# Twelve tiles of the last count on GpSimd and ScalarE, an early first norm, a separate tile for the first mixture's norms, a third bank for the last experts, and a refitted timetable

## The chip, the cores and the metric

One NeuronCore of a Trainium2 chip runs the whole program. The metric is the device time of one execution in microseconds. The engines are TensorE (PE; PEld is its weight load), VectorE (DVE), ScalarE (ACT), GpSimd (POOL) and SyncE (SP), each with its own in-order instruction stream; they meet only in semaphores.

## The reference, cut to what matters

Eight batches (B = 8) of 512 rows of 128 numbers go through two layers. Each layer has a modulation `mod` from `c @ wmod` and is x + gate * f(scale * norm(x) + shift), twice. In short:

```python
# layer 0, attention: 8 heads of 16
scores = q @ k.T * 0.25 * 1.25
threshold = top_k(scores, 102)[0][..., -1:]          # per row, the 102nd largest
scores *= where(scores >= threshold, 1.24, 1.0)
li = conv3(scores.mean(axis=-2))                      # one factor per key and head
ctx = softmax(scores * li) @ v;  out = ctx @ Wo + bo
# layer 0, mixture: x = res + n + (n @ mix_w + mix_b), then 8 experts, top 2 by softmax
y_e = silu(n @ w1[e] + b1[e]) @ w2[e] + b2[e];  out = sum_e combine[:, e] * y_e
# layer 1, state space: in_proj, conv4, silu, x_proj, softplus; 512 steps of
h = exp(dt * A) * h + dt * b * x;  y = h . c + D * x   # 256 channels x 16 states
# layer 1, mixture: top 2 of 8 experts, at most 153 rows an expert, rows gathered and scattered
y_e = (gelu-like)(x @ w_gate[e]) * (x @ w_c_fc[e]) @ w_c_proj[e]
```

The threshold of each of 32 tiles (8 heads x 4 blocks of 128 queries, 128 x 512 scores each) is found by search: a tile's scores are compared with a guess, the hits of each row are counted, and the guess is moved. After three rounds the fourth and last count leaves the number of scores at or over the last guess and the mask of them.

## The kernel before

The work is written as 29 small threads (Python generators), each bound to one engine, each running over the eight batches. `weave` (L2096) puts them into the engines' streams: it keeps a planned clock for each engine, takes the time after each `yield` of a number as the duration of what was just issued and a `yield` of a semaphore value as a wait, and always issues the piece with the earliest planned start. Of pieces that start within `NEAR` of each other the one that is due first by `TIMETABLE` (L50) goes first. So the order on each engine is fixed when the program is built, by planned and not by real times.

A batch goes through these stages:

- prepare: `dve_norm` (L485; statistics, reciprocal root on GpSimd by `pool_norm`, normalised tile), `pe_prepare` and `act_prepare` for keys, queries and values. Queries and keys are split into three bf16 parts each (`dve_prepare`), written to memory and read back stacked (`sp_stack`).
- refill: `pe_refill`, `act_refill`: 32 score tiles, scaled by each row's length, as f16 (`z_at`).
- search: `act_search` (L776) and `dve_search` (L790), four rounds. In rounds 0, 1, 2 ACT does 8, 14, 14 of the 32 tiles with Sign and a sum, DVE the others; in the fourth (k = 3) DVE does all 32 (`SIGNS`, L39).
- choice: `pe_choice`, `dve_choice`, `pool_choice`: the exact threshold and mask weights, 32 tiles.
- softmax: `pe_softmax`, `act_softmax`, `dve_softmax`, then `pe_project`; `attended` ends attention.
- mixture 0: `dve_mixture0` (L1269), `pe_mixture0`, `act_mixture0`: three norms in bank `side`, router, split; then `pe_experts0`, `act_experts0`, `pool_experts0`: 32 expert steps, in each a matmul up, Silu on ACT, a product on POOL (L1413), a matmul down.
- states: `dve_mamba`, `dve_states` and partners: 32 scans.
- mixture 1: `dve_mixture1` routes, `pool_mixture1` scatters the rows of `rest.nrm` to memory with eight indirect DMAs (L1765, signal `sent_in`), `pe_mixture1` reads them back turned; `pe_experts1` (L1777), `act_experts1`, `dve_experts1`: 32 steps over two banks; then `res_rows`, store, eight gathers on POOL (`pool_finish`, L1897), and `dve_finish` (L1887) adds them and sends the batch out.

Attention of one batch runs beside everything behind attention ("rest") of the batch before. Both have their own banks (`att.bank`, `rest.bank`) and tiles, each four banks of 128 x 512 f32. All three norms of mixture 0 and both of layer 1 write the same tile `rest.nrm`; so `dve_mixture0` waits for `shares` and `sent_in` of the batch before, and `pe_mixture0` for `tok`.

Before the threads start, `sp_setup`, `pool_setup`, `act_setup`, `pe_setup` (L389) and `dve_setup` (L398) run: loads in SP's queue, constants, both layers' modulation; `started` (L460) makes each engine wait for all of it. `pool_one_hots` stands first in `pool_rest`, with a planned 20.0.

Of the kernel before, what the change touches and what calls it, by code (L numbers as in the profile page):

```python
# [11 lines left out]
B, S, D = 8, 512, 128  # L12
P = 128
# [25 lines left out]
SIGNS = (8, 14, 14, 0)  # L39
SLOPE = 1.0 / 140.0  # L40
# [8 lines left out]
PERIOD = 363.6  # L49
TIMETABLE = {  # L50
    "pe_rest": (155.6425, (1727.5, 3672.5, 2524.5)),
    "act_rest": (83.2100, (3233.2, 3240.1, 2778.8)),
    "dve_rest": (110.8225, (2583.4, 3814.2, 3934.2)),
    "pool_rest": (118.1500, (0.0, 1840.0, 357.8)),
    "sp_rest": (15.3000, (3830.8, 3231.2, 5913.4)),
    "pe_mixtures": (10.3100, (4106.7, 4650.2, 5749.5)),
    "act_mixtures": (2.7000, (2555.5, 2487.3, 2054.2)),
    "dve_mixtures": (18.7400, (2279.9, 3457.5, 4617.6)),
    "pool_mixtures": (3.1800, (3586.9, 4341.6, 4427.8)),
    "dve_finishes": (2.8800, (6003.9, 4512.4, 4461.6)),  # L60
    "pool_finishes": (9.0400, (4205.9, 3170.0, 4019.7)),
    "sp_finishes": (0.9000, (5331.9, 7065.6, 6229.8)),
    "pe_choices": (42.2400, (2470.1, 2031.9, 620.0)),
    "act_choices": (2.5600, (4613.2, 4593.8, 3374.6)),
    "dve_choices": (58.8100, (1867.1, 2951.7, 2585.9)),
    "pool_choices": (21.4400, (2700.2, 3240.7, 4358.6)),
    "pe_attention": (57.4700, (4549.4, 4490.0, 4186.3)),
    "act_attention": (76.9400, (3555.2, 3778.3, 4824.6)),
    "dve_attention": (104.6500, (5209.4, 3457.4, 3015.7)),
    "pool_attention": (6.4600, (3316.0, 4230.4, 5170.6)),  # L70
    "sp_attention": (10.3500, (3385.9, 2184.6, 2995.6)),
    "pe_prepares": (9.0800, (2715.0, 4201.9, 1888.5)),
    "act_prepares": (2.9000, (5207.8, 5106.6, 2033.5)),
    "dve_prepares": (16.2500, (7193.4, 6820.5, 7496.6)),
    "pe_refills": (12.8000, (3056.0, 3617.0, 4283.2)),
    "act_refills": (19.2000, (1273.8, 220.9, 1809.4)),
    "sp_rows": (0.3937, (3488.0, 2251.9, 2327.0)),
    "sp_ups": (10.6875, (5049.3, 5188.3, 4982.0)),
    "sp_downs": (7.0875, (5306.5, 3602.3, 3452.1)),
# [51 lines left out]
def emit(nc, ctx, A, out):  # L131
# [40 lines left out]
    siluc, modp, bop, ready = sig("siluc", 2), sig("modp", 2), sig("bop"), sig("ready", 5)  # L172
# [98 lines left out]
    aim, signed, counted = sig("aim", ROUNDS), sig("signed", sum(SIGNS)), sig("counted")  # L271
# [30 lines left out]
    hid = [flat(hfc2)[:, wide + u * CAP:wide + (u + 1) * CAP] for u in range(2)]  # L302
# [4 lines left out]
    ccs = [sb(f"ccs{i}", [P, S]) for i in range(3)]  # L307
    spreadsBC = nc.dram_tensor("spreads", (2 * NS, S), F32, kind="Internal").ap()
# [36 lines left out]
    def pool_setup():  # L345
# [26 lines left out]
        built.up(pool.iota(spare[:], pattern=[[P, PICKS]], base=SLOTS, channel_multiplier=1))  # L372

# [1829 lines left out]
```

## Time and profile before

| | us |
|---|---|
| median of three timed runs | 2922.21 (2920.47 to 2929.23) |
| the profiled execution | 2924.21 |
| its span, first to last instruction | 2923.0 |
| busy: PE / DVE / ACT / POOL | 2182 / 2338 / 1463 / 1190 |

The mean granted clock of TensorE was 0.874 of full speed. The profile gives busy time by engine; the chain that ended last, followed back from the last instruction; groups of instructions by line, with the idle time before them and what released them; and instructions in order of time. A TensorE instruction of f32 counts as two passes (x2). The durations that overlap the next instruction's start are pipelined: a count on DVE is 742 ns long, but the next one starts 667 ns after it.

### The profile page before, as it was taken

The numbers are of one execution on the slowest core, as the hardware profiler recorded it, in microseconds if no ns is written. First come the engines' busy times: TensorE is split into PE (matmuls) and PEld (weight loads), VectorE is DVE, ScalarE is ACT, GpSimd is POOL, SyncE is SP. The second block draws the span as 40 slices with busy tenths as digits, with TensorE's granted clock in tenths as the row PEclk, the third lists the DMA queues.
The fourth block names the chain that finished last, engine by engine and source line by source line (L and its number), as shares of the span: only waits on it lengthen the run. The fifth ranks groups of instructions, "written<-read, shape, count | busy, mean of one in ns | idle before, by whom it ended". The sixth has DMA issues, their size and how long they took to land.

```text
span 2923.0 us, 33653 instructions
## 1 busy us (share of the span) xinstructions
PE 2182.0 (75%) x8767; PEld 1101.9 (38%) x8767; DVE 2338.2 (80%) x6145; ACT 1463.2 (50%) x3124; POOL 1189.6 (41%) x1118
## 2 busy tenths in 40 slices
PE   4169776978778876888679876888769887778645
PEld 2016222553234522554235522454235532355214
DVE  5884898979898798978998798978989788953472
ACT  2406723766166733767056742757146751644323
POOL 2020253615454253725445152724445163724461
PEclk8589798999989998989989999989989898789757
DMA  4001112242043312233033321333133321313223
GB/s 107 0 15 36 29 37 85 80 107 75 27 122 71 104 50 72 91 96 93 27 107 75 105 60 54 109 78 103 31 97 83 101 63 39 113 38 111 83 75 95
DMA packets 137459, 215.11 MB, mean 74 GB/s; under 512 B 17872, under 2 KB 57440, under 8 KB 134112
## 3 DMA queue, kind: packets, MB, share of 16 engines
q1 hardware_dynamic: 133088, 203.88, 24.2%
q0 software_dynamic: 4096, 8.40, 0.9%
q14 instruction: 204, 1.67, 0.2%
q8 instruction: 71, 1.16, 0.2%
HBM read 190.06 MB, written 22.15 MB: 73 GB/s over the span
## 4 chain that ended last, share of the span: by engine, by line
DVE 35%; issue 19%; PE 19%; POOL 10%; ACT 9%; DVEq 4%; DMA 3%; SPq 1%; POOLq 0%; ACTq 0%
DVE wmask L804 10%; DVE best L946 6%; DVEq L948 4%; POOL gat L1649 4%; PE ps_att L1064 3%; ACT wmask L786 2%; POOL slots L1765 2%; PE ps_rest L1353 2%; PE ps_rest L1439 2%; PE ps_att L1075 2%; PE ps_rest L1792 1%; DVE pick L953 1%; POOL rest_c L1662 1%; POOL rest_c L1649 1%; DVE hg L1621 1%
## 5 line engine op out<-in xcount | busy, mean ns | idle before, releaser
L1413 POOL TENSOR_TENSOR gat<-sil,cbs 128x512 f32<-128x512 f32 x256 | 324.4, 1271 | 137.0 <-ACT sil L1378 74.2
L1378 ACT ACTIVATE sil<-ps_rest,w_b1T 128x512 f32<-128x512 f32 x256 | 175.3, 685 | 383.3 <-PE ps_rest L1353 369.9
L804 DVE TENSOR_SCALAR_CACHE_REDUCE wmask<-z,tc 128x512 bf16<-128x512 f16 x512 | 345.8, 742 | 18.3 <-ACT z L771 15.6
L980 POOL TENSOR_SCALAR wmask<-wmask 128x512 bf16<-128x512 bf16 x256 | 158.2, 618 | 412.4 <-DVE wmask L937 409.2
L1064 PE MATMUL ps_att<-z,Vp 128*32 128x128 f32 x2048 | 277.3, 280 | 13.1 <-DVE z L1136 13.1
L1353 PE MATMUL ps_rest<-rest_hT,WF 128*128 128x512 f32 x512 | 281.5, 636 | 0.0
L1343 PE MATMUL ps_rest<-gat,WP 128*128 128x512 f32 x512 | 269.3, 608 | 15.6 <-POOL gat L1413 15.4
L737 PE MATMUL ps_att<-qk 128*128 128x512 bf16 x512 | 227.8, 465 | 45.7 <-DMA qk<-bounce 27.1
L1064 PEld LDWEIGHTS ps_att<-z,Vp 128*32 128x32 f32 x2048 | 206.4, 111 | 124.5 <-issue 115.1
L1592 ACT ACTIVATE ps_rest<-cols,Aneg 128x512 f32<-128x512 f32 x256 | 173.3, 681 | 100.6 <-DVE hg L1621 91.2
L1075 PE MATMUL ps_att<-ident,z 128*128 128x128 f32 x1024 | 172.4, 293 | 63.6 <-ACT z L1093 40.1
L1649 POOL TENSOR_TENSOR gat<-cols,cbs 128x512 f32<-128x512 f32 x128 | 162.7, 1271 | 139.8 <-DVE cols L1530 139.8
L1114 DVE CUSTOM_DVE_ANT_0 z<-ps_att,wmask 128x512 f32<-128x512 f32 x256 | 174.3, 681 | 52.1 <-PE ps_att L1052 45.8
L1662 POOL TENSOR_TENSOR rest_c<-rest_c,hg 128x512 f32<-128x512 f32 x128 | 162.1, 1267 | 128.5 <-DVE hg L1621 128.4
L937 DVE SCALAR_TENSOR_TENSOR wmask<-ps_att,g_v,wmask 128x512 bf16<-128x512 f32 x256 | 192.1, 750 | 27.4 <-DVE pick L953 21.0
L1569 PE MATMUL ps_rest<-hg,ident 128*128 128x512 f32 x256 | 166.6, 737 | 58.5 <-DVE hg L1621 58.5
L1093 ACT ACTIVATE z<-z,nmx 128x512 f32<-128x512 f32 x256 | 184.9, 722 | 17.3 <-POOL row_scale L655 7.5
L890 PE MATMUL ps_att<-wmask,Qpad 128*64 128x512 bf16 x256 | 102.3, 415 | 115.1 <-POOL wmask L980 92.0
L506 POOL TENSOR_TENSOR rest_rstd<-rest_vpe,halfs 128x4 f32<-128x4 f32 x40 | 40.7, 1016 | 357.1 <-DVE rest_vpe L494 357.1
L946 DVE MAX8 best<-ps_att 128x8 f32<-128x512 f32 x256 | 176.5, 690 | 3.9 <-PE ps_att L874 3.9
L1621 DVE TENSOR_TENSOR hg<-ps_rest,ccs 128x512 f32<-128x512 f32 x256 | 173.6, 681 | 5.0 <-PE ps_rest L1569 5.0
L1792 PE MATMUL ps_rest<-cols,WF 128*128 128x153 f32 x512 | 131.2, 340 | 51.9 <-DVE gat L1871 27.0
(348 smaller groups left out, 4810.8 us busy)
## 6 DMA issues: line engine op xcount, KB each, us to landing
cbs<-spreads SPq DMA_DIRECT2D x128, 256.0 KB, 3.6
ccs<-spreads SPq DMA_DIRECT2D x128, 256.0 KB, 3.3
WF<-in_w SPq DMA_DIRECT2D x64, 256.0 KB, 2.7
WP<-in_w SPq DMA_DIRECT2D x64, 256.0 KB, 2.7
WF<-in_wfc SPq DMA_DIRECT2D x64, 256.0 KB, 2.7
WG<-in_wgate SPq DMA_DIRECT2D x64, 256.0 KB, 3.0
WP<-in_wproj SPq DMA_DIRECT2D x64, 256.0 KB, 3.1
qk<-bounce SPq DMA_DIRECT2D x32, 384.0 KB, 4.9
```

Source lines behind the costliest of these rows:

```text
L737: return pe.matmul(bank[:], qs[:, h, j * P:(j + 1) * P], ks[:, h, :], start=True, stop=stop)
L804: od.up(dve.tensor_scalar(wmask[:, i, :], z_at[i], tc[:, 0, i:i + 1], None, ALU.is_ge, ALU.add, accum_out=tc[:, 1, i:i + 1]))
L937: masked.up(dve.scalar_tensor_tensor(wmask[:, i - 1, :], xbank[(i - 1) % 3][:], g_["v"][:, i - 1:i], wmask[:, i - 1, :], ALU.is_ge, ALU.add))
L946: od.up(dve.max(best[u][:, 0:8], xbank[i % 3][:]))
L1064: mm = pe.matmul(obank[o:o + 32, a * P:(a + 1) * P], Vp[:, kc, h, :], pT[u][:, kc, :], start=kc == 0, stop=kc == NT - 1)
L1075: mm = pe.transpose(in_tiles(tbank)[:, kc, :], prob[n % 2][:, kc * P:(kc + 1) * P], ident[:])
L1343: down0.up(pe.matmul(bk[3][:], W2[e % 2][:, c, :], gat[(n - 3) % 2], start=False, stop=False))
L1353: up0.up(pe.matmul(bk[n % 2][:], W1[e % 2][:, c * P:(c + 1) * P], rest.hT[:], start=True, stop=True))
L1413: weighed0.up(pool.tensor_tensor(gat[m % 2], sil[m % 2], cbs[e % 2][:], ALU.mult))
L1621: seen.up(dve.tensor_tensor(hc[k], dA[m % 3][:], ccs[s % 3][:], ALU.mult))
L1649: inputs.up(pool.tensor_tensor(dBx[2 * k + s % 2], dtx[:, k, :], cbs[s % 4][:], ALU.mult))
L1662: addedY.up(pool.tensor_tensor(rest.c[2][:], rest.c[2][:], hc[1], ALU.add))
```

## The change

- The last count: `SUMS = 12`. A new thread part `pool_search` compares the last 12 tiles with their guesses on POOL, writing only the mask; `act_search` then copies each mask onto itself on ACT with a sum; DVE counts the first 20 tiles and waits for `signed.all(b)`. The new signal is `cut`.
- The first norm of batch 0: it moves from the threads into the setup functions, on DVE, POOL and PE; its rows are loaded ahead of `wmod`. The modulation of layer 1 moves to `dve_late` (`dve_modulation`), and `started` waits for three instead of five `ready`.
- The three norms of mixture 0 write `mix_nrm`, which is the tile `ccs[2]` of the state stage. The waits of `dve_mixture0` and `pe_mixture0` for the batch before change; the wait for `sent_in` moves to `dve_mamba`, the one for `shares` further down.
- In the last batch the experts of layer 1 use three banks instead of two (`ups_of`), and a third tile `hid`.
- The planned durations of many pieces, the `TIMETABLE`, `PERIOD` and `NEAR` have other values; only examples stand below. Planned times in it are not instructions, but they decide the order.

```diff
+SUMS = 12
-PERIOD = 363.6
+PERIOD = 218.6
-    "dve_rest": (110.8225, (2583.4, 3814.2, 3934.2)),
-    "pool_rest": (118.1500, (0.0, 1840.0, 357.8)),
+    "dve_rest": (104.8950, (7361.2, 9520.1, 6636.9)),
+    "pool_rest": (113.4225, (3646.3, 5783.0, 5981.8)),
-    "dve_choices": (58.8100, (1867.1, 2951.7, 2585.9)),
-    "dve_attention": (104.6500, (5209.4, 3457.4, 3015.7)),
-    "pool_attention": (6.4600, (3316.0, 4230.4, 5170.6)),
+    "dve_choices": (58.8100, (10295.5, 8638.1, 9066.7)),
+    "dve_attention": (93.0000, (9927.1, 8799.5, 8058.7)),
+    "pool_attention": (14.0075, (10939.3, 9640.5, 9278.9)),
...
+    hid = [...] + [flat(sil2)[:, wide:wide + CAP]]
+    mix_nrm = in_tiles(ccs[2])
 sp_setup
+        xin[0].up(sp.dma_start(xr[0][:], A["x"][0].rearrange("(j p) d -> p j d", p=P)))
         loaded.up(sp.dma_start(wmod, A["wmod"].rearrange("l p n -> p l n")))
-        xin[0].up(sp.dma_start(xr[0][:], A["x"][0].rearrange("(j p) d -> p j d", p=P)))
 pool_setup, at its end
+        pool.wait_ge(*built.all(0))
+        for _ in pool_norm(att, 0, 0):
+            pass
 pe_setup
-        for l in range(2):
+        for l, bank in enumerate((att.bank[2], rest.bank[2])):
...
+            if l == 0:
+                bop.up(pe.matmul(rest.bank[3][:, 0:1], wts["Wo"][:], wts["bv"][:], start=True, stop=True))
+                pe.wait_ge(*built.at(0, 1))
+                for _ in pe_norm(att, 0, 0, att.bank[0]):
+                    pass
 dve_setup
+        dve.wait_ge(*xin[0].at(0))
+        for _ in dve_norm(att, 0, 0, xr[0]):
+            pass
...
+        dve_modulation(0, att.bank[2])
 dve_late
+        dve_modulation(1, rest.bank[2])
 act_search, after its rounds
+        for n in range(SUMS):
+            i = TILES - 1 - n
+            yield cut.at(b, n)
+            act.wait_ge(*cut.at(b, n))
+            signed.up(act.activation(wmask[:, i, :], wmask[:, i, :], ACT.Copy, accum_out=tc[:, 1, i:i + 1]))
+            yield 0.71
+    def pool_search(b):
+        yield aim.at(b, ROUNDS - 1)
+        pool.wait_ge(*aim.at(b, ROUNDS - 1))
+        for n in range(SUMS):
+            i = TILES - 1 - n
+            cut.up(pool.tensor_scalar(wmask[:, i, :], z_at[i], tc[:, 0, i:i + 1], None, ALU.is_ge))
+            yield 0.64
 dve_search
-            for i in range(TILES - SIGNS[k]):
+            for i in range(TILES - (SUMS if last else SIGNS[k])):
...
+            if last:
+                yield signed.all(b)
+                dve.wait_ge(*signed.all(b))
 pe_mixture0
-            yield tok.at(b - 1, 2)
-            pe.wait_ge(*tok.at(b - 1, 2))
+            yield rest.normed.at(b - 1, 4)
+            pe.wait_ge(*rest.normed.at(b - 1, 4))
+            yield lg_ps.at(b - 1, 1)
+            pe.wait_ge(*lg_ps.at(b - 1, 1))
 dve_mixture0
-            yield shares.at(b - 1)
-            dve.wait_ge(*shares.at(b - 1))
-            yield sent_in.all(b - 1)
-            dve.wait_ge(*sent_in.all(b - 1))
-        yield from dve_norm(rest, b, 0, xr[b % 3])
+            yield rest.normal.all(b - 1)
+            dve.wait_ge(*rest.normal.all(b - 1))
+        yield from dve_norm(rest, b, 0, xr[b % 3], mix_nrm)
 dve_mamba, ahead of its norm
+        if b:
+            yield sent_in.all(b - 1)
+            dve.wait_ge(*sent_in.all(b - 1))
+    def ups_of(b):
+        return rest.bank[0:2] + ([rest.bank[3]] if b == B - 1 else [])
 pe_experts1; the same in act_experts1 and dve_experts1
-                if n >= 2:
-                    yield joined.at(b, n - 2)
-                    pe.wait_ge(*joined.at(b, n - 2))
+                if n >= len(ups):
+                    yield joined.at(b, n - len(ups))
+                    pe.wait_ge(*joined.at(b, n - len(ups)))
 dve_states, the scan
-                yield 1.22
+                yield 1.15
 dve_finish
-                yield 0.36
+                yield 0.62
 pool_attention
             yield from pool_prepare(b)
+            yield from pool_search(b)
-    NEAR = 0.135
+    NEAR = 0.158
```

## Rows read from the trace of the kernel before

**Rows 1.** Chain that ended last, in order of time: start us, us, what.

```profile
114.18 21.43 DVE wmask L804 x64
...
704.43 21.43 DVE wmask L804 x64
...
2374.10 21.44 DVE wmask L804 x64
```

**Rows 2.** Busy time by stretch: stretch and us, then busy us by engine.

```profile
core 0: us, PE busy (x) PEld busy (x) DVE busy (x) ACT busy (x) POOL busy (x), PEclk, DMA share, GB/s
704.43:1039.61 335.18, 267.87 (x1092) 135.19 (x1091) 291.06 (x749) 181.50 (x391) 147.65 (x137) 0.90 0.28 79
...
2600.00:2923.00 323.00, 195.43 (x693) 108.95 (x692) 142.77 (x300) 110.27 (x203) 135.27 (x117) 0.76 0.30 90
```

**Rows 3.** The same view: one last count, the choice behind it, batch 0's last count.

```profile
1039.60:1061.10 21.50, 13.05 (x31) 5.41 (x29) 21.46 (x65) 6.24 (x10) 10.44 (x9) 0.88 0.25 75
1061.10:1125.00 63.90, 49.80 (x137) 14.17 (x137) 57.38 (x147) 7.20 (x11) 29.05 (x39) 0.93 0.11 31
...
114.18:135.70 21.52, 0.00 (x0) 0.00 (x0) 21.49 (x65) 0.00 (x0) 0.00 (x0) 0.50 0.00 0
```

**Rows 4.** Timeline of POOL and of PE around 1051 to 1067 us.

```profile
1051.10 1.26 POOL L1413 TENSOR_TENSOR gat<-sil,cbs 128x512 f32<-128x512 f32 x1 [0.45 <-PE ps_rest L1343]
...
1067.18 0.61 POOL L980 TENSOR_SCALAR wmask<-wmask 128x512 bf16<-128x512 bf16 x1 [13.10 <-DVE wmask L937]
...
1061.63 0.26 PE L862 MATMUL ps_att<-g_bad,ones_col 128*1 128x32 f32 x2 [8.98 <-DVE g_bad L827]
```

**Rows 5.** Groups by line: busy us, mean ns of one, idle before it.

```profile
L1413 POOL TENSOR_TENSOR gat<-sil,cbs 128x512 f32<-128x512 f32 x256 | 324.4, 1271 | 137.0 <-ACT sil L1378 74.2 <-PE ps_rest L1343 47.6 <-ACT cbs L1387 11.9
...
L804 DVE TENSOR_SCALAR_CACHE_REDUCE wmask<-z,tc 128x512 bf16<-128x512 f16 x512 | 345.8, 742 | 18.3 <-ACT z L771 15.6
...
L980 POOL TENSOR_SCALAR wmask<-wmask 128x512 bf16<-128x512 bf16 x256 | 158.2, 618 | 412.4 <-DVE wmask L937 409.2
...
L786 ACT ACTIVATE wmask<-att_c,tc 128x512 bf16<-128x512 f16 x96 | 68.6, 723 | 25.2 <-DVE tc L853 25.1
```

**Rows 6.** Timeline of ACT and of DVE at the end of a third round.

```profile
1033.07 0.21 ACT L786 ACTIVATION_READ_ACCUMULATOR wmask<-both_parts,tc 128x1 f32 x1
...
1031.49 5.40 DVE L1887 SCALAR_TENSOR_TENSOR xr<-cols,sv_p,xr 128x128 f32<-128x128 f32 x8
```

**Rows 7.** Timeline: first statistics of mixture 0 twice, then what the last experts0 await.

```profile
1278.44 0.87 DVE L487 BATCH_NORM_STATS2 rest_stats<-xr 128x6 f32<-128x128 f32 x4 [1.63 <-DMA slots<-rest_nrm,goes]
...
2610.16 0.87 DVE L487 BATCH_NORM_STATS2 rest_stats<-xr 128x6 f32<-128x128 f32 x4 [8.96 <-DMA slots<-rest_nrm,goes]
...
2662.15 0.68 DVE L1192 TENSOR_TENSOR cpart<-cres,cmid 32x512 bf16<-32x512 f32 x1
...
2663.78 0.28 ACT L1858 ACTIVATE cols<-ps_rest 72x128 f32<-72x128 f32 x1
```

**Rows 8.** Timeline of the start.

```profile
12.23 5.26 PE L394 MATMUL ps_att<-w_cT,z 128*128 128x8 f32 x24 [12.23 <-ACT w_cT L386]
...
19.86 0.87 DVE L487 BATCH_NORM_STATS2 att_stats<-xr 128x6 f32<-128x128 f32 x4 [0.19 <-DVE gbo L424]
...
26.05 1.05 POOL L506 TENSOR_TENSOR att_rstd<-att_vpe,halfs 128x4 f32<-128x4 f32 x1
...
29.73 2.08 PE L570 MATMUL ps_att<-att_hT,w_Wk 128*128 128x512 f32 x2 [0.95 <-ACT att_hT L482]
...
57.52 2.66 PE L737 MATMUL ps_att<-qk 128*128 128x512 bf16 x5 [13.31 <-DMA qk<-bounce]
```

**Rows 9.** DMA issues in the first 60 us: times, KB, median us to landing.

```profile
xr<-in_x SPq DMA_DIRECT2D x3, 256.0 KB, 4.9
```

**Rows 10.** Busy time by stretch: one expert (four steps) of the last batch.

```profile
2877.37:2882.04 4.67, 3.84 (x24) 3.23 (x24) 2.12 (x6) 2.42 (x6) 0.00 (x0) 1.00 0.53 155
```

**Rows 11.** Timeline of POOL where gathers stand between products.

```profile
1019.40 0.98 POOL L1897 DMA_INDIRECT cols<-results,slot  x1 [0.16 <-issue]
1020.40 1.27 POOL L1413 TENSOR_TENSOR gat<-sil,cbs 128x512 f32<-128x512 f32 x1
```

More of the change, by code:

```diff
@@ L270, in emit @@
     raw, zed = sig("raw", TILES), sig("zed", TILES)
-    aim, signed, counted = sig("aim", ROUNDS), sig("signed", sum(SIGNS)), sig("counted")
+    aim, signed, counted = sig("aim", ROUNDS), sig("signed", sum(SIGNS) + SUMS), sig("counted")
+    cut = sig("cut", SUMS)
     tallied, ranked = sig("tallied"), sig("ranked")
@@ L301, in emit @@
     acts = [flat(sil2)[:, 0:wide], flat(hfc2)[:, 0:wide]]
-    hid = [flat(hfc2)[:, wide + u * CAP:wide + (u + 1) * CAP] for u in range(2)]
+    hid = [flat(hfc2)[:, wide + u * CAP:wide + (u + 1) * CAP] for u in range(2)] + [flat(sil2)[:, wide:wide + CAP]]
     xpad = [sb(f"xpad{k}", [P, 3 + S]) for k in range(DC)]
@@ L465, in started, with pe_norm @@
         eng.wait_ge(*loaded.all(0))
-    def pe_norm(w, b, k, bank, whole=False):
+    def pe_norm(w, b, k, bank, whole=False, nrm=None):
         for j in range(NT):
@@ L566, in pe_prepare @@
             pe.wait_ge(*masked.all(b - 1))
-        yield from pe_norm(att, b, 0, bk[0])
+            yield from pe_norm(att, b, 0, bk[0])
         yield att.normed.at(b)
@@ L650, in pool_prepare @@
     def pool_prepare(b):
-        yield from pool_norm(att, b, 0)
+        if b:
+            yield from pool_norm(att, b, 0)
         yield lens.at(b)
@@ L663, in dve_rows @@
             dve.wait_ge(*counted.at(b - 1))
-        yield from dve_norm(att, b, 0, xr[b % 3])
+            yield from dve_norm(att, b, 0, xr[b % 3])
     def dve_values(b):
@@ L1225, in pe_mixture0 @@
         if b:
-            yield tok.at(b - 1, 2)
-            pe.wait_ge(*tok.at(b - 1, 2))
-        yield from pe_norm(rest, b, 0, side)
+            yield rest.normed.at(b - 1, 4)
+            pe.wait_ge(*rest.normed.at(b - 1, 4))
+            yield lg_ps.at(b - 1, 1)
+            pe.wait_ge(*lg_ps.at(b - 1, 1))
+        yield from pe_norm(rest, b, 0, side, False, mix_nrm)
         yield rest.normed.at(b, 0)
@@ L1232, in pe_mixture0 @@
         yield 1.25
-        yield from pe_norm(rest, b, 1, side, True)
+        yield from pe_norm(rest, b, 1, side, True, mix_nrm)
         yield rest.normed.at(b, 1)
@@ L1241, in pe_mixture0 @@
         yield 1.25
-        yield from pe_norm(rest, b, 2, side, True)
+        yield from pe_norm(rest, b, 2, side, True, mix_nrm)
         yield rest.normed.at(b, 2)
@@ L1289, in dve_mixture0 @@
         dve.wait_ge(*turned_back.at(b, 1))
-        yield from dve_norm(rest, b, 2, in_tiles(side))
+        yield from dve_norm(rest, b, 2, in_tiles(side), mix_nrm)
         yield lg_ps.at(b, 0)
         dve.wait_ge(*lg_ps.at(b, 0))
+        if b:
+            yield shares.at(b - 1)
+            dve.wait_ge(*shares.at(b - 1))
         od.up(dve.tensor_reduce(sv["m"][:], logits0, AX.X, ALU.max)); od.settle()
```

157 lines of the change are left out of this document (80 added, 77 removed).

## The prediction

> **What bounds the kernel now.** I read the chain that ended last first. It holds the same block eight times, DVE's last count of a batch: 64 pieces (32 tiles, each a count and the read of its accumulator) in 21.43 us, 0.67 us for a tile, with nothing between them [rows 1]. From one block to the next it is about 334 us in the middle of the run (704.43 to 1039.61 is the period of [rows 2]; there are six, 331 to 335), and 549 us from the last one to the end. So there are three parts: a start in which batch 0's attention runs alone, seven blocks of overlapped work, a tail in which batch 7's experts and state scan run alone.
>
> The busy times of one period [rows 2] say that DVE is the fullest engine: 291.1 us of 335.2 (87%), PE 267.9, ACT 181.5, GpSimd (POOL) 147.7. In the tail it is nobody: DVE 142.8 of 323. DVE is thus close to the bound in the middle, with 44 us of short waits for other engines, and dependences set the tail.
>
> Three stretches around one last count [rows 3] show what is free there. In the 21.5 us of the count DVE is full (21.46), POOL has 10.4 us of work (eight expert products), ACT 6.2, PE 13.1. PE then stands still for 8.98 us and POOL for 13.10 us until the count is over [rows 4]: their in-order streams have the choice stage next. At batch 0 nobody but DVE works during the block (the last line of [rows 3]).
>
> **The last count.** Removed: 12 of DVE's 32 counts, 12 x 0.67 = 8.0 us a batch. DVE's share becomes 20 x 0.67 = 13.4 us. Added: 12 comparisons on POOL, and 12 copies with a sum on ACT, each behind its comparison. The trace has neither. The nearest for the first is POOL's one-input pass over the same 128x512 bf16 tile, 618 ns [rows 5], 12 x 0.62 = 7.4 us; for the second the Sign pass with its sum over such a tile, 723 ns, with the read of the sum mostly under the next pass: 12 x 0.72 = 8.7 us. With both engines free the last sum is there 0.62 + 8.7 + 0.2 = 9.5 us after the thresholds, before DVE's 13.4: the whole 8.0 us is gained. That is batch 0.
>
> The Trainium skill (GPSIMD Engine Reference, the introduction) calls GpSimd the wrong choice for ordinary elementwise arithmetic, with VectorE roughly twice as fast; its section 4.1 limits that to two inputs. This trace has the one-input tile at 618 ns on POOL beside 742 on DVE [rows 5], so the first sentence does not hold for this shape. By it a comparison would take about 1.48 us and the twelve 17.8 us, an estimate from that page and DVE's row, and even batch 0 would gain only about 3 us.
>
> In batches 1 to 7 POOL also has the experts of the batch before, 1.27 us a product [rows 5], and both stand in one in-order queue. All twelve comparisons first: DVE's 13.4 us decide, gain 8.0. All eight products of that stretch too: 10.4 + 7.4 + 0.9 (ACT's last copy and read) = 18.7, gain 2.7. One comparison behind each product: 12 x (1.27 + 0.62) + 0.9 = 23.6, a loss of 2.2. Which order comes out is the planner's doing. It counts an expert step as two matmuls of 1.09, 2.18 us, and a product as 1.30, which leaves 0.88; a comparison is written at 0.64, the rest, 0.24, is more than NEAR (0.158), so that often a second one starts there and pushes the product back. The timetable lets products go first when both are ready (pool_rest 3646 to 5982, pool_attention 10939 to 9279). That is about 1.3 comparisons a step, 9.2 steps, and on the chip 9.2 x 1.27 + 7.4 + 0.9 = 20.0 us: gain 1.4. During such a wait DVE can do other work. The residual sums of the batch before (5.4 us, L1887) now fill the wait for ACT in the third round: ACT's last sign was read at 1033.3, DVE came out of L1887 at 1036.8 [rows 6]. If they move into the new wait, the third round ends up to 3.5 us earlier; I take 3.1. Together 4.5 us a batch; the ends are -2.2 and 8.0. Seven batches: 31.5 us. With batch 0's 8.0: 39.5.
>
> What hides the added work: the 13.10 us that POOL idles behind its products, and ACT's 15 idle us of 21.5. Queued behind the comparisons on POOL are expert products; PE waits for them, but it has the 8.98 us it lost before. If that cover is too small the experts end later, which is a rival below.
>
> **The first mixture's norms in their own tile.** DVE no longer waits for the scatter to read rest_nrm. In the middle that wait costs 1.63 us of idle DVE, in the tail 8.96 us [rows 7]. But the next experts also need the result rows of the batch before. In the tail the last write of the router's split starts at 2662.15 and the rows are copied at 2663.78 [rows 7]; the rows are what is late next. So not 9 us but the little by which the last-but-one experts get easier: I take 3 (0 to 6). In each of six middle periods 1 us (0 to 3): 6. The wait for sent_in moves to the norm ahead of the state scan, when the scatter is long past: nothing. Two waits of PE are exchanged for earlier ones: nothing.
>
> **Early first norm.** Now: matmuls with wmod from 12.23, modulation on DVE, statistics at 19.86, POOL's root only at 26.05 because the one-hot masks stand ahead of it, the normed tile used by PE at 29.73, first scores at 57.52 [rows 8]. After: statistics as soon as the rows have landed. They are issued at 7.5 us and take about 4.9 to land [rows 9], so 12.4; statistics 1.4, root 1.05, normalising 1.1: 16.0; then the modulation of layer 0 alone and its bias, 2.2: 18.2; ACT 0.8: 19.0, and PE has done the second layer's matmuls by 19.5. Against 29.73 now that is 10 us earlier. The transfer of the split keys then starts at 27, where the engines still move late weights; I take off 1: 9 us, range 5 to 11. The second modulation (1.7 us) goes where DVE waits for scores until 59: nothing.
>
> **Third bank for the last experts.** One expert takes 4.67 us, PE is busy for 3.84 of them, DVE 2.12, ACT 2.42 [rows 10]. With a third bank PE is next: at most 0.83 x 8 = 6.6 us; I take 6 (0 to 7). Weight transfers get 0.8 us less to land.
>
> **Durations, timetable, NEAR.** No instruction changes; orders may. Most durations come closer to the rows (scan 1.22 to 1.15, choice of finish 0.36 to 0.62 against 0.69 measured). Bounds: the 44 us of waits in a period [rows 2] could shrink or grow. With no reason for a sign I take zero, and 2 us a period either way in the range.
>
> **The sum.** 39.5 + 9 + 6 + 3 + 6 = 63.5. The profiled execution took 2924.2 (span 2923.0); 2924.2 - 63.5 = 2860.7. It was 2.0 above the median of the three timed runs, 2922.2, so the forecast is 2859 us, its own range 2842 to 2876. A measurement of this kernel tells about 0.3% (9 us) from no change.
>
> **Rivals.**
> 1. The comparisons go first everywhere, 8.0 us in each batch: 7 x 3.5 = 24.5 more, 2834. For it: POOL and PE idle 13 and 9 us in just this stretch, so the experts need not be late. Against it: the timetable's order for POOL.
> 2. The gain is given back before the experts' output. The products pushed back by 7.4 us fall into the choice stage, where PE has 49.8 us of work in 63.9 [rows 3]; DVE's choice then waits for PE. The seven batches give nothing: 63.5 - 31.5 = 32, so 2890. Against it: 14 us of PE are free there.
> 3. One comparison behind each product: 23.6 us a count, 6.7 worse than my 4.5, 7 x 6.7 = 47 more, 2906. POOL's stream does alternate like this in the stretch where its eight gathers stand between products [rows 11].
> 4. Slower. The comparisons fall into that very pace: 0.16 + 0.98 + 1.27, measured start to start 2.43 us a product, instead of 1.27 + 0.45 = 1.72 [rows 4, 11], because the gathers and the comparisons share the gaps. Then 12 x 2.43 + 0.9 = 30.1 us a count, 8.7 worse than now, 7 x 8.7 = 61, against the other gains of 32: +29, 2951. It decides from 26.0 us a count on (4.6 worse x 7 = 32), or 2.1 us a step.
> 5. The change does not do what it says: the count shrinks on DVE, but refitted orders use up all of it. About 2920.
>
> **Chances.** Forecast 0.43; rival 1 0.22; rival 2 0.16; rival 3 0.11; rival 4 0.05; rival 5 0.03. Faster by over 0.3%: 0.92, within 0.3%: 0.03, slower: 0.05. The range takes in rival 1 with 12 us below it for the six periods' 2 us (2822) and ends at rival 3 (2906).
>
> **What would show it.** The blocks of 64 pieces become 40 pieces in 13.4 us. If rival 1 holds, DVE goes on at once into the flags; if my 20 us, an idle DVE or L1887 stands there, with ACT's sum as releaser. POOL's comparison should take 0.6 us, ACT's sum 0.72, and the period should be 329 us (326 under rival 1, 333 under 2, 335 under 3). First scores at 48.5 instead of 57.5. An expert in the last batch 3.9 us. A POOL comparison near 1.5 us, a period above 334, or PE waiting for POOL products throughout the choice stage would make the forecast wrong.

## The result

The changed kernel takes 2952.68 us, the median of 4 runs (2950.31 to 2955.68), beside 2921.34 for the kernel before on the same chip (2918.80 to 2929.23). The ratio is 1.0102, with a 95% interval of 1.0086 to 1.0118: 1.0% slower. The forecast was 2859 us with a range of 2822 to 2906. The profiled execution took 2955.68 us, its span is 2954.4 and the mean granted clock of PE 0.872 (0.874 before).

### The profile page after: what moved, and what is told of

Same layout as the page of the kernel before. It is cut to its first block, busy times and chain, and to the rows that moved or that the text cites. A ratio compares the mean times of both kernels' runs of the same rounds, so it can differ in the third digit from the quotient of the medians.

```text
span 2954.4 us, 33658 instructions
## 1 busy us (share of the span) xinstructions
PE 2182.0 (74%) x8649; PEld 1101.5 (37%) x8767; DVE 2269.8 (77%) x5953; ACT 1525.2 (52%) x3316; POOL 1337.1 (45%) x1214
## 3 DMA queue, kind: packets, MB, share of 16 engines
q8 instruction: 71, 1.16, 0.2%
## 4 chain that ended last, share of the span: by engine, by line
DVE 37%; issue 18%; PE 17%; POOL 14%; ACT 7%; DVEq 4%; another core or an unknown queue 2%; DMA 1%; SPq 0%; POOLq 0%; ACTq 0%
DVE ps_rest L1649 6%; DVE best L980 6%; DVEq L982 4%; POOL gat L1450 4%; POOL wmask L818 3%; DVE wmask L835 3%; DVE hg L1661 3%; PE ps_att L1098 2%; DVE z L1148 2%; POOL slots L1805 2%; ACT wmask L803 2%; POOL cols L1943 2%; DVE pick L987 1%; PE ps_rest L1390 1%
## 5 line engine op out<-in xcount | busy, mean ns | idle before, releaser
L835 DVE TENSOR_SCALAR_CACHE_REDUCE wmask<-z,tc 128x512 bf16<-128x512 f16 x512 | 345.8, 741 | 19.5 <-ACT z L788 16.5
L1380 PE MATMUL ps_rest<-gat,WP 128*128 128x512 f32 x512 | 284.5, 639 | 82.1 <-POOL gat L1450 81.9
L1390 PE MATMUL ps_rest<-rest_hT,WF 128*128 128x512 f32 x512 | 294.2, 662 | 2.2 <-ACT sil L1415 2.2
L1014 POOL TENSOR_SCALAR wmask<-wmask 128x512 bf16<-128x512 bf16 x256 | 158.2, 618 | 267.2 <-DVE wmask L971 263.6
L754 PE MATMUL ps_att<-qk 128*128 128x512 bf16 x470 | 192.7, 434 | 43.7 <-DMA qk<-bounce 25.9
L1943 POOL DMA_INDIRECT cols<-results,slot x64 | 63.0, 985 | 319.6 <-DMA results<-cols 309.6
L980 DVE MAX8 best<-ps_att 128x8 f32<-128x512 f32 x256 | 176.5, 689 | 3.1 <-PE ps_att L908 3.0
L1380 PEld LDWEIGHTS ps_rest<-gat,WP 128*128 128x128 f32 x512 | 92.6, 198 | 225.0 <-POOL gat L1450 185.6
```

The costliest lines, as they stand in the source:

```text
L754: return pe.matmul(bank[:], qs[:, h, j * P:(j + 1) * P], ks[:, h, :], start=True, stop=stop)
L835: od.up(dve.tensor_scalar(wmask[:, i, :], z_at[i], tc[:, 0, i:i + 1], None, ALU.is_ge, ALU.add, accum_out=tc[:, 1, i:i + 1]))
L980: od.up(dve.max(best[u][:, 0:8], xbank[i % 3][:]))
L1380: down0.up(pe.matmul(bk[3][:], W2[e % 2][:, c, :], gat[(n - 3) % 2], start=False, stop=False))
L1390: up0.up(pe.matmul(bk[n % 2][:], W1[e % 2][:, c * P:(c + 1) * P], rest.hT[:], start=True, stop=True))
```

## The profile after

The first part of the page, busy time by engine. Before it was 2182, 2338, 1463 and 1190 us for PE, DVE, ACT and POOL:

```profile
PE 2182.0 (74%) x8649; PEld 1101.5 (37%) x8767; DVE 2269.8 (77%) x5953; ACT 1525.2 (52%) x3316; POOL 1337.1 (45%) x1214
```

DVE lost 68 us and POOL gained 147.5. The change adds 8 x 12 = 96 instructions to POOL, so each costs 1.54 us. The groups by line, one form each (columns as in [rows 5]), say it directly:

```profile
L818 POOL TENSOR_SCALAR wmask<-att_c,tc 128x512 bf16<-128x512 f16 x32 | 49.7, 1556 | 85.3 <-DVE tc L887 85.3
...
L1014 POOL TENSOR_SCALAR wmask<-wmask 128x512 bf16<-128x512 bf16 x256 | 158.2, 618 | 267.2 <-DVE wmask L971 263.6 <-ACT sil L1415 0.4
...
L810 ACT ACTIVATE wmask<-wmask 128x512 bf16<-128x512 bf16 x96 | 60.4, 629 | 136.1 <-POOL wmask L818 136.1
```

L818 is the new comparison: 1556 ns. It takes 1550 to 1577 ns in each of its 96 places, in batch 0 as in the middle, so that the experts' work beside it has no part in its price. L1014 is the pass of [rows 5] (L980 before), still 618 ns; the prediction had taken its price for the comparison. ACT's sum (L810) waits 136 us in all for POOL, and for nothing else.

Four stretches of the changed kernel (columns as in [rows 2]): batch 0's last count, a middle one with its wait, the choice behind that, and the last batch's experts.

```profile
107.00:127.50 20.50, 0.27 (x2) 0.09 (x2) 14.43 (x46) 8.67 (x24) 18.50 (x12) 0.50 0.00 0
1047.00:1076.00 29.00, 15.08 (x31) 5.11 (x31) 14.36 (x45) 14.23 (x34) 28.83 (x21) 0.91 0.16 45
1076.00:1139.00 63.00, 47.69 (x132) 13.92 (x135) 56.84 (x143) 7.20 (x11) 29.83 (x40) 0.96 0.11 31
2893.00:2929.00 36.00, 27.87 (x179) 25.68 (x180) 15.64 (x39) 16.97 (x46) 0.00 (x0) 0.94 0.43 132
```

In the second line POOL is full, 28.83 of 29.0 us, where [rows 3] had 10.44 of 21.50; DVE, full before, has 14.36. The bound of the stage has moved from DVE to POOL. The stretch ends 1 us behind the wait; from the first count to DVE's first piece behind the wait it is 28.0 us where it was 21.5, and the same to 0.1 us in all seven batches. In batch 0 it is 19.3. The choice behind it takes 63 us as before (63.9). POOL's and DVE's timelines in that stretch:

```profile
1047.00 1.56 POOL L818 TENSOR_SCALAR wmask<-att_c,tc 128x512 bf16<-128x512 f16 x1 [2.65 <-DVE tc L887]
1048.55 1.25 POOL L1450 TENSOR_TENSOR gat<-sil,cbs 128x512 f32<-128x512 f32 x1
1049.80 3.09 POOL L818 TENSOR_SCALAR wmask<-att_c,tc 128x512 bf16<-128x512 f16 x2
1052.87 1.25 POOL L1450 TENSOR_TENSOR gat<-sil,cbs 128x512 f32<-128x512 f32 x1
...
1071.03 3.09 POOL L818 TENSOR_SCALAR wmask<-both_parts,tc 128x512 bf16<-128x512 f16 x2
...
1060.35 0.09 DVE L835 DVE_READ_ACCUMULATOR wmask<-both_parts,tc 128x1 f32 x1
1074.97 0.20 DVE L855 TENSOR_SCALAR ps_att<-tc 128x32 int32<-128x32 f32 x1 [14.53 <-ACT wmask L810]
```

One or two comparisons stand between products: twelve comparisons and seven products, 12 x 1.55 + 7 x 1.25 = 27.3 us, and ACT's last sum behind them. DVE ends its 20 tiles at 1060.4 and stands still for 14.53 us; in batch 0 this wait is 5.85 us.

The start of the changed kernel, PE's first scores and POOL's first comparisons:

```profile
49.00 1.06 PE L754 MATMUL ps_att<-qk 128*128 128x512 bf16 x2 [14.99 <-DMA qk<-bounce]
...
107.24 6.20 POOL L818 TENSOR_SCALAR wmask<-att_c,tc 128x512 bf16<-128x512 f16 x4 [67.41 <-DVE tc L887]
```

First scores come at 49.00 instead of 57.52 [rows 8]; batch 0's last count starts at 107 instead of 114 [rows 1].

Each batch has one last count. The whole run can be read from the starts of these eight on DVE: the distance from the first to the second, six periods from there to the eighth, and what follows to the end of the span. All are in us. The later kernels are those of the next section.

| kernel | first last count at | to the second | a period (mean of six) | from the eighth to the end |
|---|---|---|---|---|
| before | 114.2 | 256.9 | 333.8 | 548.9 |
| after | 107.3 | 255.6 | 339.8 | 552.6 |
| e4_same_order | 106.6 | 256.3 | 332.5 | 550.8 |
| e2_cheap | 106.7 | 249.4 | 326.3 | 548.3 |
| e8_sign_first | 107.4 | 249.8 | 326.7 | 545.9 |
| e11_sign_and_later | 106.9 | 249.9 | 326.8 | 533.7 |
| e10_near_only | 113.8 | 257.1 | 333.0 | 561.1 |
| e1_no_share | 107.7 | 254.8 | 376.0 | 555.6 |
| e3_told | 107.3 | 256.5 | 391.6 | 599.2 |

## The experiments

Sharing stands here for the last count divided between DVE and the pair of GpSimd and ACT. Two theories stood first. Theory S: the sharing fails by the price of GpSimd's comparison alone. Theory O: the refitted order, or contention, has taken the gain. The runs separate the price, the order and the other parts.

**What sets GpSimd's price: p0_forms and p1_forms2.** In batch 0's start, where POOL is idle, forms of one instruction run over a 128x512 tile, one after the other, each twice (`c` is a pointer to a column, `pf` f16, `pb` and `qb` bf16, `qf` f16 out):

```diff
+step.up(pool.tensor_scalar(qb, pf, c, None, ALU.is_ge))            # p0_forms L824, and 15 more
+step.up(pool.tensor_scalar(qb, pb, 0.25, None, ALU.mult))          # L829
+step.up(pool.tensor_scalar(qb, pf, 0.25, 0.5, ALU.mult, ALU.add))  # L831
```

> The changed kernel with 32 extra passes (16 forms, twice) on GpSimd while it idles in batch 0's start; they write tiles that nobody reads yet. Each is one input of 128x512 and one output. Which part of the comparison (f16 in, pointer scalar, is_ge, one operation instead of two) makes it 1.55 us where the weighing pass (bf16, mult and add with constants) takes 0.62? Theory A, the type: every pass with f16 in takes 1.55 us and every bf16 pass 0.62, whatever the operation. Theory B, the operation: every is_ge takes 1.55 us, also bf16 with a constant, and mult with a pointer stays at 0.62. Theory C, the pointer scalar: all with a pointer 1.55, all with constants 0.62. The total time says nothing here.

The groups of p0_forms by line:

```profile
L824 POOL TENSOR_SCALAR cbs<-cbs,pc 128x512 bf16<-128x512 f16 x2 | 3.1, 1572 | 0.2
...
L829 POOL TENSOR_SCALAR cbs<-cbs 128x512 bf16<-128x512 bf16 x2 | 3.0, 1488 | 0.2
...
L831 POOL TENSOR_SCALAR cbs<-cbs 128x512 bf16<-128x512 f16 x2 | 1.2, 618 | 0.2
L832 POOL TENSOR_SCALAR cbs<-cbs 128x512 f16<-128x512 f16 x2 | 1.2, 618 | 0.2
```

Thirteen forms with one operation take 1486 to 1593 ns, whatever the operation (is_ge, mult, subtract, max), the types (f16, bf16, f32) and the operand: a constant 1486 to 1488, a pointer 1560 to 1593. The three with the pair mult and add take 618, f16 input included. So neither the type nor the comparison makes the price. Is any second operation enough?

> The same place for 15 other forms on GpSimd, 128x512 each, after the first look: there every pass of one operation took 1.49 us (constant) or 1.56 to 1.59 (pointer scalar), whatever type and operation, and the pass mult-then-add with two constants 0.62, also with f16 in. Theory A, the number of operations: each form of two operations takes 0.62, so that is_ge with a pointer and a second operation (times 1, plus 0) would be 0.62 too. Theory B, the pair: only mult-then-add with constants is fast and all others take 1.5 us or more. Theory C, the pointer: two operations are fast only with constants, is_ge among them. A difference of two tensors (bf16, f16) is there for comparison: 1.3 us like the product by each theory.

POOL's timeline in p1_forms2; all lines have f16 in and bf16 out. The operations, from the code: L824 is_ge then mult, L827 mult then add with one pointer, L828 the same with two, L832 add then mult, L834 mult then is_ge, L837 mult then subtract.

```profile
40.27 2.01 POOL L824 TENSOR_SCALAR cbs<-cbs,pc 128x512 bf16<-128x512 f16 x1
...
46.49 0.69 POOL L827 TENSOR_SCALAR cbs<-cbs,pc 128x512 bf16<-128x512 f16 x1
47.29 0.76 POOL L828 TENSOR_SCALAR cbs<-cbs,pc 128x512 bf16<-128x512 f16 x1
...
53.06 0.65 POOL L832 TENSOR_SCALAR cbs<-cbs 128x512 bf16<-128x512 f16 x1
...
55.81 1.93 POOL L834 TENSOR_SCALAR cbs<-cbs 128x512 bf16<-128x512 f16 x1
...
62.02 1.93 POOL L837 TENSOR_SCALAR cbs<-cbs 128x512 bf16<-128x512 f16 x1
```

Of the pairs tried only mult with add, in either order, with constants or pointers, is fast: 0.62 to 0.76 us. Every other pair tried takes 1.92 to 2.01. No form with a comparison in it takes under 1.48 us. Why the pair is fast is not shown. The two programs took 2958.46 and 2956.90 us, one run each.

**Without the sharing, planned anew: e1_no_share.** DVE counts all 32 tiles again and `pool_search` is gone; the rest of the change stays.

```diff
-SUMS = 12
+SUMS = 0
 pool_attention
-            yield from pool_search(b)
```

> The changed kernel with the last count given back to DVE alone (SUMS = 0, no comparisons on GpSimd); everything else of the change stays, its timetable too. Theory 1, the price of the comparison is all that went wrong: each of seven counts is 21.5 us instead of 28.9, batch 0's 21.5 instead of 20.3, so 2953 - 52 + 1 = 2902 us, faster than before by the early norm and a little of the tail. Rival 2, the refitted orders cost time by themselves: 2921 us or more.

3173.84 us, ratio 1.0835 (1.0815 to 1.0856): 270 us over what was expected. The same stretch, one period, of this kernel and then of e4_same_order, which does the same work in the order of the changed kernel:

```profile
1111.50:1489.40 377.90, 280.33 (x1092) 141.74 (x1091) 290.55 (x749) 183.91 (x391) 147.56 (x136) 0.82 0.25 70
```

```profile
1032.30:1364.70 332.40, 264.87 (x1078) 134.94 (x1092) 290.21 (x750) 181.84 (x391) 148.02 (x137) 0.90 0.29 80
```

DVE's work is equal (290.55 and 290.21 us), the period 45.5 us longer, and PE's granted clock 0.82 instead of 0.90, with PE busy for 74% of the period instead of 80%. One place where the time goes is the wait before the products of the experts, in the groups by line of that period, e1_no_share first:

```profile
L1450 POOL TENSOR_TENSOR gat<-sil,cbs 128x512 f32<-128x512 f32 x32 | 40.5, 1267 | 49.0 <-ACT sil L1415 32.0 <-PE ps_rest L1380 14.8 <-ACT cbs L1424 1.7
```

```profile
L1448 POOL TENSOR_TENSOR gat<-sil,cbs 128x512 f32<-128x512 f32 x33 | 41.8, 1271 | 11.6 <-PE ps_rest L1378 6.8 <-ACT sil L1413 2.4 <-ACT cbs L1422 2.0
```

GpSimd's idle time ahead of them is 49.0 us instead of 11.6. Attention suffers too: from DVE's ranks, made at the start of the choice, to its end it is 275 us in batches 1 to 6 (258 to 281), where e4_same_order has 202. The planner, given other work with the same timetable, has made an order with longer waits; which piece in it is misplaced was not traced. This run therefore says nothing on the sharing. It says that a comparison of two kernels of this kind must keep the order, and the next runs do.

**The true price told to the planner: e3_told.**

```diff
 pool_search
-            yield 0.64
+            yield 1.55
```

> The changed kernel with the planner told the measured duration of the comparison (1.55 instead of 0.64), so that the order on all engines is planned anew. Theory 1: GpSimd's own work in the stage (12 x 1.55 = 18.6 us beside products of 1.27) cannot be planned away: one comparison behind each product gives 12 x 2.82 = 34 us a count, up to 5 us worse each, 2950 to 2990. Rival 4, the wrong planned duration is the cause and a planner that knows it finds an order without loss: 2925 or less.

3312.50 us, ratio 1.1313 (1.1287 to 1.1339), again far over what was expected. One of the six periods:

```profile
1149.90:1542.10 392.20, 280.61 (x1092) 135.48 (x1091) 285.58 (x726) 191.77 (x414) 166.45 (x149) 0.83 0.25 68
```

The truth about one duration, with the 29 lines of the timetable left as they were, costs 360 us more than the wrong number did. Part of it stands in the count stage: the new order puts one or two products behind each comparison, 18 in all instead of seven, and in the middle it is 40.5 us from the first count to DVE's next piece, 12.5 more than in the changed kernel, of a period that is 52 us longer. The rest was not traced.

**The same work as before in the new order: e4_same_order.** The planner still sees the sharing; what is issued is DVE's 12 counts.

```diff
 act_search, pool_search: the yields stay, no instruction is issued
-            act.wait_ge(*cut.at(b, n))
-            signed.up(act.activation(wmask[:, i, :], wmask[:, i, :], ACT.Copy, accum_out=tc[:, 1, i:i + 1]))
...
-            cut.up(pool.tensor_scalar(wmask[:, i, :], z_at[i], tc[:, 0, i:i + 1], None, ALU.is_ge))
 dve_search, last round
-                dve.wait_ge(*signed.all(b))
+                for i in range(TILES - SUMS, TILES):
+                    od.up(dve.tensor_scalar(wmask[:, i, :], z_at[i], tc[:, 0, i:i + 1], None, ALU.is_ge, ALU.add,
+                                            accum_out=tc[:, 1, i:i + 1]))
```

> The changed kernel with each engine's order kept as it is (the planner still counts the comparisons and sums at their durations), but none of them is issued: DVE counts all 32 tiles again, the last twelve where it waited for the sums. It takes away what the earlier run without the share changed on the side, the order planned anew. Theory 1, the price: every count 21.5 us (now 28.9 in seven batches, 20.3 in the first): 2953 - 52 + 1 = 2902 us. Rival, the timetable's orders cost time by themselves: 2921 or more, and the 3174 us of the earlier run were not only the anew planned order.

2911.32 us, ratio 0.9953 (0.9934 to 0.9971): 14 us faster than before, where 24 were expected. The expectation took the changed kernel's stage as 28.9 us, and 20.3 in batch 0, 1 us too long each. With 28.0 and 19.3 the changed kernel loses 7 x 6.5 - 2.2 = 43 us in its count stages. Against the changed kernel (1.0102) the sharing itself costs 1.49% of 2925, about 44 us. The spans say the same (2954.4 and 2908.9), and the table puts 43.0 of the 45.5 us between the first and the eighth last count, 7.3 in each of six periods. So what the sharing costs is what its count stages are longer by, and theory O falls: the new order alone isn't slower.

**The sharing at the forecast's price: e2_cheap.** The order stays. GpSimd runs the 618 ns pass instead of the comparison. The last comparison of 12 tiles is left out, and their counts are set to a number inside the window.

```diff
-            cut.up(pool.tensor_scalar(wmask[:, i, :], z_at[i], tc[:, 0, i:i + 1], None, ALU.is_ge))
+            cut.up(pool.tensor_scalar(wmask[:, i, :], wmask[:, i, :], -0.5, 0.5, ALU.mult, ALU.add))
 dve_search, last round
+                od.up(dve.memset(tc[:, 1, TILES - SUMS:], 98.0))
```

> The changed kernel, every instruction in its place, but GpSimd's comparison replaced by a pass that the trace has at 0.62 us (the old mask of the third round times -0.5 plus 0.5, bf16), and one tiny memset that puts 98 in place of the twelve counts. What is left out: the last comparison of 12 of 32 tiles. Theory 1: a pass takes 0.62, a count stage with its seven products 7 x 1.27 + 12 x 0.62 + 0.9 = 17.2 us instead of 28.9, batch 0's 13.5 instead of 20.3: 2953 - 82 - 7 = 2864 us, about what was forecast. Rival 3, the gain is given back by experts that end later: the count stage shrinks the same, but the period stays over 333 us and the time over 2900.

2864.44 us, ratio 0.9784 (0.9766 to 0.9803): as expected. But for the memset only the price of 96 instructions differs from the changed kernel: 96 x (1.55 - 0.61) = 90 us, and the two lie 0.0318 x 2928 = 93 us apart. The middle count, as a stretch:

```profile
1010.00:1028.00 18.00, 13.56 (x32) 4.84 (x31) 14.64 (x48) 13.79 (x34) 17.77 (x21) 1.00 0.24 72
```

Even so POOL is full, 17.77 of 18.0. From the first count to DVE's next piece it is 16.5 us. DVE's first piece after its counts waits 3.13 us for ACT's sum in this kernel (14.53 in the changed one).

**The whole result with the cheap pass: e8_sign_first.** ACT takes the sign of threshold minus score with its sum, as in the rounds before, straight from the scores. GpSimd turns the sign into the mask with the fast pair, two slots later. PE waits for that mask in the choice only, and DVE turns the 12 sums into counts. The planned order is that of the changed kernel.

```diff
 act_search
-            signed.up(act.activation(wmask[:, i, :], wmask[:, i, :], ACT.Copy, accum_out=tc[:, 1, i:i + 1]))
+            signed.up(act.activation(wmask[:, i, :], z_at[i], ACT.Sign, scale=-1.0, bias=tc[:, 0, i:i + 1],
+                                     accum_out=tc[:, 1, i:i + 1]))
 pool_search, for tile m = n - 2
...
+                pool.wait_ge(*signed.at(b, sum(SIGNS) + m))
+                halved.up(pool.tensor_scalar(wmask[:, i, :], wmask[:, i, :], -0.5, 0.5, ALU.mult, ALU.add))
 pe_choice
+                    pe.wait_ge(*halved.at(b, TILES - 1 - i))
```

> The changed kernel in its order, the last count's share done the other way round: ACT first takes Sign and sum of z against the threshold, as in the rounds before, so that the count needs nothing of GpSimd; GpSimd then makes the mask of it with the 0.62 us pass (times -0.5 plus 0.5), two places later in its own stream, and PE waits for it in the choice stage. Theory 1: DVE waits for ACT's last Sign; with GpSimd at 12 x 0.62 and its products in the same stream the stage takes about 17 us: 2955 - 82 - 7, about 2865, with the reference's result. Rival: ACT behind its Silu becomes the bound, or GpSimd stalls for each Sign: stage 22 us or more, 2900 or more.

2863.63 us, ratio 0.9786 (0.9768 to 0.9804): 2.1% faster than before. A middle count as a stretch, and DVE's and POOL's timelines in it:

```profile
1013.80:1032.00 18.20, 14.88 (x36) 5.01 (x36) 16.49 (x55) 14.81 (x35) 16.81 (x20) 1.00 0.23 71
```

```profile
1027.12 0.08 DVE L839 DVE_READ_ACCUMULATOR wmask<-both_parts,tc 128x1 f32 x1
1027.80 0.17 DVE L851 TENSOR_SCALAR tc<-tc 128x12 f32<-128x12 f32 x1 [0.60 <-ACT wmask L811]
...
1027.30 2.36 POOL L821 TENSOR_SCALAR wmask<-wmask 128x512 bf16<-128x512 bf16 x4
1029.63 2.48 POOL L1458 TENSOR_TENSOR gat<-sil,cbs 128x512 f32<-128x512 f32 x2
```

DVE waits 0.60 us instead of 14.53: the counts no longer hang on POOL, whose last masks are made while DVE already works on the flags. The stage is 14.0 us, 2.5 shorter than in e2_cheap, and yet the two kernels take the same time (ratios 0.9786 and 0.9784, periods 326.7 and 326.3). So these 2.5 us a batch do not show in the time; where they go was not traced.

**The last experts: e9_down_later and e12_two_banks.** In the changed kernel an expert of the last batch, from the third on, still takes 4.67 us, from the first matmul of one expert to that of the next. PE's timeline:

```profile
2906.32 0.42 PE L1836 MATMUL ps_rest<-cols,WF 128*128 128x153 f32 x2
...
2909.84 1.31 PE L1850 MATMUL ps_rest<-sil,WP 128*128 128x153 f32 x8 [1.16 <-DVE sil L1924]
2910.99 0.42 PE L1836 MATMUL ps_rest<-cols,WF 128*128 128x153 f32 x2
```

PE runs the four steps without a gap, and then waits 1.16 us for the last product of the expert ahead before the matmul down, which stands at a fixed place in its stream. e9_down_later moves it one step back, and ACT's reading of its result too:

```diff
+        late_by = 8 if b == B - 1 else 7
...
-            if n >= 7 and (n - 7) % FC == 0 and (n - 7) // FC < E:
+            if n >= late_by and (n - late_by) % FC == 0 and (n - late_by) // FC < E:
```

> The changed kernel, with the down matmul of each expert of the last batch one step later (and ACT's reading of it too). In the changed kernel an expert still takes 4.67 us there with the third bank: PE stands 1.16 us before each down matmul for DVE's doubled tile. Theory 1, this place in PE's stream closes the loop and not the banks: an expert takes 3.9 to 4.2 us, 8 x 0.6, 2947 to 2950 us, 3 to 6 us less than the changed kernel. Rival, weights landing or ACT bound the expert: 4.6 us or more and 2953.

2951.10 us, ratio 1.0087 (1.0069 to 1.0105), beside 1.0102: in the time the difference is inside the intervals. In the trace the wait before the matmul down is gone but for the last two experts (0.56 and 0.83 us). An expert takes 3.2 us where PE isn't stopped; weight transfers stop it in three of them, once for 1.39 us. From PE's first matmul of these experts to the end of the run it is 56.1 us instead of 61.1. That profiled execution had lost 4 us ahead of the stage.

e12_two_banks undoes the third bank in the changed kernel:

```diff
-        return rest.bank[0:2] + ([rest.bank[3]] if b == B - 1 else [])
+        return rest.bank[0:2]
```

> The kernel after with two banks for the last batch's experts, as before the change. The prediction booked the third bank at 6 us (0 to 7): then this is 6 us above the kernel after, ratio 1.0123, some 2962. By what the trace of after shows (an expert still 4.67 us, the stage 34 to 35 us instead of 36 to 37) it is 0 to 2 us above, ratio 1.010 to 1.011, some 2953 to 2956. An expert takes 4.67 us in both theories' low case; 5.4 would be needed for the 6 us.

2955.44 us, ratio 1.0103 (1.0085 to 1.0121): no difference from the changed kernel. PE's timeline with two banks:

```profile
2905.51 0.53 PE L1836 MATMUL ps_rest<-cols,WF 128*128 128x153 f32 x2 [0.38 <-DVE gat L1917]
...
2906.75 0.53 PE L1836 MATMUL ps_rest<-cols,WF 128*128 128x153 f32 x2 [0.46 <-DVE gat L1917]
...
2907.45 1.31 PE L1850 MATMUL ps_rest<-sil,WP 128*128 128x153 f32 x8
...
2912.13 1.31 PE L1850 MATMUL ps_rest<-hfc,WP 128*128 128x153 f32 x8
```

An expert takes 4.68 us here too. With two banks PE waits twice for a bank and not before the matmul down; with three it waits once, 1.16 us, before the matmul down. The third bank has moved the wait. What little it brings is mostly in the first expert (3.97 us instead of 4.62): from PE's first matmul to the end of the run it is 61.1 us with the bank and 62.2 without.

**Both improvements: e11_sign_and_later,** which is e8_sign_first with the edit of e9_down_later.

> e8_sign_first with the last batch's down matmuls one step later. If the 2 us of e9_down_later are real and add up: 0.9786 minus 0.0007, that is 2862 to 2864 beside 2926 of the kernel before, the count stage unchanged at 14 to 15 us. Rival: the shift meets the weight transfers again and nothing is gained, 0.979 to 0.980. Should the order planned for the rest change by this, over 0.985.

2852.79 us, ratio 0.9758 (0.9735 to 0.9781), the fastest of these kernels, 2.4% below the kernel before. The step from e8_sign_first is 0.0028, as large as its uncertainty. In the trace PE's stage of the last experts takes 35.9 us instead of 40.8; 7 us less between the last count and them are not explained. What is late next in the stage is a weight transfer, as two lines of PE show:

```profile
2810.53 0.50 PE L1845 MATMUL ps_rest<-cols,WF 128*128 128x153 f32 x2 [1.03 <-DMA WG<-in_wgate]
...
2811.12 1.21 PE L1859 MATMUL ps_rest<-sil,WP 128*128 128x153 f32 x8
```

**How touchy the order is: e10_near_only,** the kernel before with one number of the planner changed.

```diff
-    NEAR = 0.135
+    NEAR = 0.158
```

> The kernel before with one number of the planner changed, NEAR 0.135 to 0.158: no instruction, operand or wait is added or removed, only the order in each engine's stream may differ. The prediction booked the refit at 0, within 2 us a period, so within 14 us (2926 plus or minus 14 here). Rival: the fitted constants belong to one exact program, and a change of any of them gives an order that costs tens to hundreds of us (the re-planned e1_no_share and e3_told lay 250 and 360 us above their like): then over 2970, with ranks to attended at over 220 us instead of 204, and PE's clock below 0.87.

2932.27 us, ratio 1.0028 (1.0015 to 1.0041): inside the 14 us booked for the refit, and the rival that any change of a constant costs tens of us does not hold for this one. By the table the loss lies in the tail (561.1 instead of 548.9), not in the periods. What made e1_no_share and e3_told so slow is therefore not the changing of just any number; both change the length of a thread whose due times are in the timetable. That this is the reason was not tried further and stays open.

## Why the prediction was wrong

- **The step that failed** is the price of the comparison. "The nearest for the first is POOL's one-input pass over the same 128x512 bf16 tile, 618 ns": that pass multiplies and adds, and this pair alone is fast. The comparison takes 1.55 us, 2.5 times as much, also on bf16 and alone on an idle engine. [rows 5] showed that the pass was cheap, but not that its cheapness belonged to its operations. By the prediction's own formula for the middle, 9.2 steps x 1.27 + 12 x 1.55 + 0.9 = 31.2 us; with the seven products really there it is 28.4, measured 28.0 (a product there takes 1.25).
- **The Trainium skill** (GPSIMD Engine Reference, the introduction) makes GpSimd about twice as slow as VectorE for elementwise work. The estimate from it, 1.48 us a comparison and 17.8 for twelve, was set aside for a row of another operation; measured are 1.55 and 18.50, and of batch 0's gain, about 3 us by that estimate, 2.2. Its section 4.1, which has GpSimd at about full rate with one input, holds here for mult with add only: 0.62 us beside DVE's 0.74 for another operation.
- **The range** ended at one comparison behind each product at 0.62 us. It held both orders of the queue but one price, although the price had no row of its own. The row next to it, the product with two inputs at 1271 ns, would have been the other bound: 12 x 1.27 + 7 x 1.27 + 0.9 = 25.0 us, which is slower than the 21.5 of before.
- **Rival 4** named 2951 us, and 2952.68 came. That is luck. Its point of decision was passed, 26.0 us a count (28.0 measured), but it summed 61 us lost in seven counts and 32 won elsewhere, where 45 were lost and about 14 won. Its mechanism, that gathers and comparisons share the gaps, is not what happened. Its chance of 0.05 rested on the order alone.
- **The order of the queue** was read rightly in kind, one or two comparisons behind each product: 12 on 7 products, 1.7 each where 1.3 were worked out. At the forecast's price (e2_cheap against e4_same_order) the sharing is worth 0.0169 x 2926 = 49 us, beside 39.5 forecast: 6.9 in batch 0's distance (8.0 forecast) and 6.2 a period (4.5).
- **POOL's idle time** was read too large. Of the 13.10 us "until the count is over" [rows 4], from 1054.1 to 1067.2, only 7.0 lie ahead of the count's end at 1061.1; the rest belongs to the choice.
- **The residual sums** did not move into the new wait. They end ahead of the last count as before, and DVE stands still for the 14.53 us. The 3.1 us a batch booked for them had no ground.
- **Batch 0** gained 2.2 us in the count stage (21.5 to 19.3) instead of 8.0: 12 comparisons alone are 18.50 us, longer than DVE's 13.4, and the last sum follows them.
- **Early first norm**: 9 us forecast. First scores came 8.5 us earlier and the first last count 7 us earlier. Right.
- **Mixture norms**: the waits that were named are gone. DVE's first statistics follow the residual sum within 0.20 us in the middle (1.63 before) and at once in the tail (8.96 before). But from the end of the last attention to the first matmul up of layer 0's experts it is 64.2 us (64.4 before); the tail's 3 us did not come. The router's split, which used to end 1.0 us ahead of ACT's copy of the result rows (2662.8 and 2663.8), now ends 15.6 us ahead of it, and PE waits 0.93 us for ACT's copies as before: the rows of the batch before are what is late, as the prediction had said. The 6 us of the middle were not measured alone: a period of e4_same_order is 1.3 us shorter than before, with the refit in it.
- **Third bank**: 6 us forecast, about 1 in the trace (e12_two_banks: from the experts' start to the end 62.2 us, with the bank 61.1), and none that the times can tell. "With a third bank PE is next" took PE's busy time as the new period, and missed the fixed place of the matmul down in PE's own stream.
- **Experts given back, rival 2**: the choice takes 63 us as before, and from the ranks to the end of attention it is 202.3 us (202.5 before, means of seven batches). Nothing was given back there.

The sum after the fact, in us: sharing +44, start -8, the bank -1, and the rest, refit and norms, -4 (as what is left of the 14 of e4_same_order). That is +31.

## What to carry to other kernels

A duration belongs to the operation as well as to engine, shape and type: before work goes to an engine, look for a row with the same operation, and if there is none, let the range hold the price of the nearest slower row. Take out of a chain what is needed only later: here the count comes first and the mask is made behind it, in the cheap form. Measure a wait from instruction to instruction; read from hand-cut stretches, the count stages came out 1 us too long each, and the cost of the sharing was expected at 51 us where it is 44. In a kernel whose order is planned, keep the order fixed when one part is measured, or the new order is what gets measured.

## What the runs showed of the hardware

GpSimd's scalar-operand pass over 128x512 elements takes 0.62 to 0.76 us for mult with add, and 1.49 (constant) to 1.59 us (pointer) for any single operation tried (p0_forms), the single multiply included; other pairs take 1.92 to 2.01 us (p1_forms2). So a second operation can make it 2.4 times faster: 1488 ns for mult with a constant, 618 ns for mult with add. The input's type (f16, bf16, and f32 for the comparison) changed next to nothing. A subtraction of a bf16 tile from an f16 one took 1.15 us, less than a one-input comparison.
